# Layer norm statistics summed on four column tiles, kept as 128x128, and spread by selector matmuls

## What is computed

```
def _ln_t(v, eps=1e-05):
    m = jnp.mean(v, axis=-1, keepdims=True)
    s = jnp.var(v, axis=-1, keepdims=True)
    return (v - m) / jnp.sqrt(s + eps)
...
x = _L0_conv_ref(x, ...)                 # group norm, attention, residual
t = _to_tokens(x)                        # (8, 1024, 256)
t = t + _L1_attn_ref(_ln_t(t), ...)      # layer norm 0, causal attention
t = t + _L1_ffn_ref(_ln_t(t), ...)       # layer norm 1, top 2 of 32 experts
```

## Time and profile before

| | us |
|---|---|
| median of 3 executions | 3855.47 (3851.91 to 3858.39) |
| the profiled execution | 3846.6 |
| its span, first to last instruction | 3844.9 |
| PE busy | 3322.6 (86%) |
| DVE busy | 2186.7 (57%) |
| ACT busy | 1670.4 (43%) |
| mean granted TensorE clock | 0.896 of 2.4 GHz |

### The profile page before, as it was taken

How to read it: one execution, slowest core, us unless ns; L and a number is a source line. 1 busy time by engine, 2 the same in 40 slices (tenths; PEclk the granted TensorE clock), 3 DMA queues, 4 the chain that set the end, 5 groups by cost and what they waited for, 6 DMA issues and landing times.

```text
span 3844.9 us, 54190 instructions
## 1 busy us (share of the span) xinstructions
PE 3322.6 (86%) x17874; PEld 1820.9 (47%) x17874; DVE 2186.7 (57%) x2905; ACT 1670.4 (43%) x2604; POOL 425.7 (11%) x539
## 2 busy tenths in 40 slices
PE   5898799987998879988799788997889988899779
PEld 2344464435644356344563445534465344554347
DVE  6634585356843568445674447744567355773544
ACT  1454335533364333644236342463424634355333
POOL 0000030001300013000230002200022000320005
PEclk7798899988999889989899888998979989899889
DMA  3011340114402144021530205302142021421125
GB/s 99 1 45 34 90 137 28 45 34 110 139 7 52 26 123 126 11 57 26 140 106 17 61 18 140 99 17 61 29 138 88 18 61 43 143 70 34 45 57 165
DMA packets 151942, 263.02 MB, mean 68 GB/s; under 512 B 26832, under 2 KB 28880, under 8 KB 151504
## 3 DMA queue, kind: packets, MB, share of 16 engines
q1 hardware_dynamic: 151632, 259.15, 24.8%
HBM read 145.80 MB, written 9.44 MB: 40 GB/s over the span
## 4 chain that ended last, share of the span: by engine, by line
PE 61%; issue 14%; DVE 12%; ACT 7%; SPq 3%; DMA 2%; POOL 1%; DVEq 0%; ACTq 0%; POOLq 0%
PE ps_acc L592 8%; PE ps_two L705 7%; PE ps_one L544 7%; DVE tops L1072 6%; PE ps_two L669 6%; PE ps_acc L604 6%; PE ps_one L546 5%; PE ps_one L545 5%; PE ps_acc L544 3%; PE ps_acc L545 3%; PE ps_acc L546 3%; PE ps_one L705 3%; ACT probs L879 2%; SPq L457 2%; PE ps_two L686 1%
## 5 line engine op out<-in xcount | busy, mean ns | idle before, releaser
L1072 DVE TENSOR_REDUCE tops<-ps_two 128x2 bf16<-128x1024 f32 (+3 forms) x896 | 964.0, 1112 | 415.0 <-PE ps_two L669 247.2
L879 ACT ACTIVATE probs<-ps_two 128x1024 f32<-128x1024 f32 (+1 forms) x704 | 641.6, 961 | 234.4 <-PE ps_two L705 151.6
L669 PE MATMUL ps_two<-stacks 32*128 32x512 f32 (+3 forms) x1792 | 425.1, 506 | 178.0 <-DVE tops L1072 141.8
L705 PE MATMUL ps_two<-stacks 97*128 97x512 f32 (+3 forms) x1408 | 472.9, 442 | 67.8 <-ACT probs L879 37.7
L592 PE MATMUL ps_acc<-probs,v_sb 128*32 128x512 f32 (+3 forms) x3584 | 459.7, 587 | 0.0
L519 POOL TENSOR_TENSOR nat<-expert_sb,nat 128x256 fp32r<-128x256 f32 x512 | 386.3, 756 | 654.8 <-ACT nat L819 557.1
L705 PEld LDWEIGHTS ps_two<-stacks 97*128 97x128 f32 x1408 | 243.3, 196 | 357.4 <-ACT probs L879 184.7
L669 PEld LDWEIGHTS ps_two<-stacks 32*128 32x128 f32 x1792 | 171.5, 202 | 453.7 <-DVE tops L1072 237.0
L819 ACT CAST nat<-expert_sb 128x256 fp32r<-128x256 f32 x256 | 103.4, 407 | 630.3 <-DVE probs L1181 519.6
L604 PE MATMUL ps_acc<-probs,ones 128*32 128x512 f32 (+3 forms) x2944 | 358.4, 560 | 0.0
L525 POOL TENSOR_TENSOR act_lo<-xn,act_hi 128x2048 fp32r<-128x2048 f32 x8 | 36.1, 4511 | 2757.0 <-ACT act_hi L929 2757.0
(11 more groups left out here) (131 smaller groups left out, 4504.6 us busy)
## 6 DMA issues: line engine op xcount, KB each, us to landing
stacks<-nat SPq DMA_DIRECT2D x792, 128.0 KB, 2.4
expert_sb<-experts_dram SPq DMA_DIRECT2D x256, 256.0 KB, 2.8
probs<-gates_dram SPq DMA_DIRECT2D x512, 128.0 KB, 3.0
x_in<-x_in_dram SPq DMA_DIRECT2D x9, 1024.0 KB, 4.9
out_dram<-x_res SPq DMA_DIRECT2D x16, 512.0 KB, 2.9
probs<-mats_dram SPq DMA_DIRECT2D x1, 2048.0 KB, 9.3
gates_dram<-w_turn SPq DMA_DIRECT2D x64, 16.0 KB, 1.6
sel_w<-sel_dram SPq DMA_DIRECT2D x1, 32.0 KB, 8.4
```

The costliest lines, as they stand in the source:

```text
L669: mm = pe.matmul(acc[:, HALF * e:HALF * e + n_keys], q_st[rows, g, j, P * i:P * i + P], k_st[rows, g, j, HALF * kh:HALF * kh + n_keys], st ...
L705: mm = pe.matmul(at[:, a:HALF], k_st[0:MID + 1, g, j, P * k:P * k + P], q_st[0:MID + 1, g, j, HALF * hf + a:HALF * hf + HALF], start=True, ...
L879: done(act.activation(probs[:, n % 2, per * i:per * i + per, a:HALF], acc[:, :, a:HALF], ACT.Exp, scale=SCALE), s + (i,))
L1072: done(dve.reduce_max(tops[:, kh, 2 * pr:2 * pr + 2, i], acc[:, :, 0:cols(st, i, kh)], AX_X), s)
```

## The change

Each layer norm becomes four steps. "lna" sums the channels with column tiles: for each quarter q of the 512 tokens, `mean_w[:, 0:32]` is multiplied by 128 columns of `x_res` into partitions 32q to 32q+31 of the bank, so the 512 means lie on a 128x128 tile, each in 32 partitions. DVE copies it to `var_sb`, now 128x128. The new step "lnm" spreads it to 128x512 by four selector matmuls (`quarter_w`, 1/32 on the 32 rows of quarter q), and DVE subtracts and ACT squares as before. "lnb" sums the squares by column tiles; epsilon, ln, exp and the Newton step work on 128x128. The new step "lnr" spreads the roots by selector matmuls, and DVE multiplies `xn` by the bank. The new semaphore `scaled` tells PE that the roots are ready. Lines of the new kernel: `by_quarter` L625, `spread_out` L632, DVE copy L1151, subtractions L1157 and L1158, epsilon L1160, Newton step L1164 to L1167, multiplications L1173 and L1174.

```diff
--- before.py
+++ after.py
@@ -114,7 +114,7 @@
         steps += a[:1] + ([("down", 1)] if experts else []) + a[1:] + b[:1] + [("norm", 0, 0, 0), b[1], ("div", 0, 0, 0), b[2], ("fin", 0, 0, 0)] + b[3:]
 
         steps += c[:1] + [("norm", 0, 1, 0), c[1], ("div", 0, 1, 0), c[2], ("fin", 0, 1, 0), c[3]] + self.out(0, 0)
-        steps += [c[4], ("lna", 0, 0), c[5], ("lnb", 0, 0), c[6], c[7], ("parts", 0)]
+        steps += [c[4], ("lna", 0, 0), ("lnm", 0, 0), c[5], ("lnb", 0, 0), c[6], ("lnr", 0, 0), c[7], ("parts", 0)]
         steps += d[:1] + [("norm", 0, 0, 1), d[1]] + self.qk(1, 0, [0]) + [("div", 0, 0, 1), d[2], ("fin", 0, 0, 1)]
         t = rows_later(self.top(1, 0, 0))
         steps += d[3:5] + spread(d[5:8] + self.v(1)[:2], t)
@@ -122,8 +122,8 @@
         e, f, g, h = (self.mix(1, g, hf, hf == g) for hf in (0, 1) for g in (0, 1))
         t = rows_later(self.top(1, 1, 0))
         steps += e[:1] + [("norm", 0, 1, 1)] + self.qk(1, 1, [0]) + [("div", 0, 1, 1), e[1], e[2], ("fin", 0, 1, 1)]
-        steps += [e[3]] + t[:3] + self.out(0, 1) + t[3:8] + [("lna", 0, 1)] + t[8:]
-        steps += f[:1] + [("norm", 1, 0, 0), ("lnb", 0, 1), f[1], f[2], ("parts", 1), ("div", 1, 0, 0)]
+        steps += [e[3]] + t[:3] + self.out(0, 1) + t[3:8] + [("lna", 0, 1)] + t[8:9] + [("lnm", 0, 1)] + t[9:]
+        steps += f[:1] + [("norm", 1, 0, 0), ("lnb", 0, 1), f[1], ("lnr", 0, 1), f[2], ("parts", 1), ("div", 1, 0, 0)]
         steps += self.qk(1, 0, [1]) + [("fin", 1, 0, 0)] + self.v(1)[2:]
         steps += spread([f[3]] + self.qk(1, 1, [1]), rows_later(self.top(1, 0, 1)))
         m = [g[1], ("div", 1, 1, 0), g[2], ("fin", 1, 1, 0)] + g[3:]
@@ -131,10 +131,10 @@
         steps += g[:1] + [("norm", 1, 1, 0)] + spread(m[:-1], t[:-1]) + [m[-1], t[-1]]
 
         steps += h[:1] + [("norm", 1, 0, 1), h[1], ("div", 1, 0, 1), h[2], ("fin", 1, 0, 1), ("stats",), h[3]]
-        steps += self.out(1, 0) + [("gn",), h[4], ("lna", 1, 0), h[5], ("split", 0), ("lnb", 1, 0), h[6], h[7]]
+        steps += self.out(1, 0) + [("gn",), h[4], ("lna", 1, 0), ("lnm", 1, 0), h[5], ("split", 0), ("lnb", 1, 0), h[6], ("lnr", 1, 0), h[7]]
         steps += [("norm", 1, 1, 1), ("div", 1, 1, 1)] + self.qk(0, 0, [0]) + [("fin", 1, 1, 1)] + self.v(0)[:2]
         steps += self.out(1, 1)
-        steps += [("split", 1), ("lna", 1, 1)] + self.qk(0, 0, [1]) + [("lnb", 1, 1)]
+        steps += [("split", 1), ("lna", 1, 1), ("lnm", 1, 1)] + self.qk(0, 0, [1]) + [("lnb", 1, 1), ("lnr", 1, 1)]
         return steps
 
     def last(self):
@@ -147,8 +147,8 @@
     return s[1] == 0 and s[3] == 0 and s[4] in (1, 2, 4, 5, 6)
 
 
-LINKS = {"stats": 3, "gn": 8, "div": 2, "lna": 1, "lnb": 5, "logits": 5}
-N_CONSTS = 15
+LINKS = {"stats": 3, "gn": 8, "div": 2, "lnm": 1, "lnb": 3, "lnr": 1, "logits": 5}
+N_CONSTS = 18
 
 
 def events(steps):
@@ -167,7 +167,7 @@
     for s in steps:
         kind = s[0]
         add(kind, s)
-        if kind in ("gn", "qk", "v", "out", "lna", "lnb", "logits", "turn", "up"):
+        if kind in ("gn", "qk", "v", "out", "lna", "lnm", "lnb", "lnr", "logits", "turn", "up"):
             use("one", s)
         if kind == "mix" and added_up(s):
             add("add", s)
@@ -285,6 +285,7 @@
         mean_w = sb("mean_w", [P, P])
         block_w = sb("block_w", [P, P])
         ones32 = sb("ones32", [P, HD])
+        quarter_w = sb("quarter_w", [P, PH, P])
 
         x_in = sb("x_in", [P, CT, T])
         x_res = sb("x_res", [P, CT, T])
@@ -302,7 +303,7 @@
         tops = sb("tops", [P, NH, G, TT], BF16)
         rsum = sb("rsum", [P, HALF])
         o_sb = sb("o_sb", [P, HALF])
-        var_sb = sb("var_sb", [P, HALF])
+        var_sb = sb("var_sb", [P, P])
         rstd = sb("rstd", [P, HALF])
         st6 = sb("st6", [P, CT, NH, 6])
         mv = sb("mv", [P, CT, 2])
@@ -366,6 +367,7 @@
         att_hi = sem("att_hi")
         att_lo = sem("att_lo")
         squared = sem("squared")
+        scaled = sem("scaled")
         gates = sem("gates")
         gates_out = sem("gates_out")
         gate_in = [sem(f"gate_in{n}") for n in range(RING)]
@@ -494,7 +496,8 @@
             pool.memset(block_w[:], 1.0 / NORM_GROUP).then_inc(consts, 1)
             pool.memset(mean_w[:], 1.0 / C).then_inc(consts, 1)
             pool.memset(ones32[:], 1.0).then_inc(consts, 1)
-            pool.wait_ge(consts, 8)
+            pool.memset(quarter_w[:], 1.0 / HD).then_inc(consts, 1)
+            pool.wait_ge(consts, 9)
             for m, value in ((ident, 1.0), (ident_bf, 1.0), (minus_bf, -1.0)):
                 pool.affine_select(out=m[:], in_=m[:], compare_op=ALU.not_equal, fill=value, base=0,
                                    pattern=[[-1, P]], channel_multiplier=1).then_inc(consts, 1)
@@ -507,7 +510,11 @@
             pool.affine_select(out=blocks, in_=blocks, compare_op=ALU.is_ge, fill=0.0, base=0,
                                pattern=[[-NORM_GROUP, P // NORM_GROUP], [0, NORM_GROUP]],
                                channel_multiplier=1).then_inc(consts, 1)
-            pool.wait_ge(consts, 14)
+            pool.affine_select(out=quarter_w[:], in_=quarter_w[:], compare_op=ALU.is_ge, fill=0.0, base=0,
+                               pattern=[[-HD, PH], [0, P]], channel_multiplier=1).then_inc(consts, 1)
+            pool.wait_ge(consts, 16)
+            pool.affine_select(out=quarter_w[:], in_=quarter_w[:], compare_op=ALU.is_ge, fill=0.0, base=HD - 1,
+                               pattern=[[HD, PH], [0, P]], channel_multiplier=-1).then_inc(consts, 1)
             pool.affine_select(out=blocks, in_=blocks, compare_op=ALU.is_ge, fill=0.0, base=NORM_GROUP - 1,
                                pattern=[[NORM_GROUP, P // NORM_GROUP], [0, NORM_GROUP]],
                                channel_multiplier=-1).then_inc(consts, 1)
@@ -610,6 +617,20 @@
                             mm = pe.matmul(ps_acc[HD * j:HD * j + HD, 1, :], ones32[:], psums[:, j, :],
                                            start=False, stop=True)
                     mm.then_inc(mixed, 1)
+
+                def by_quarter(acc, columns):
+
+                    for k in range(CT):
+                        for q in range(PH):
+                            mm = pe.matmul(acc[HD * q:HD * q + HD, 0:P], mean_w[:, 0:HD], columns(k, P * q),
+                                           start=(k == 0), stop=(k == CT - 1))
+                    return mm
+
+                def spread_out(acc, quarters):
+
+                    for q in range(PH):
+                        mm = pe.matmul(acc[:, P * q:P * q + P], quarter_w[:, q, :], quarters[:, 0:P], start=True, stop=True)
+                    return mm
 
                 def times_down(hf, j):
 
@@ -731,16 +752,16 @@
 
                         for ct in range(CT):
                             read(("out", ln, hf, ct))
-                        acc = bank(s)
-                        for k in range(CT):
-                            mm = pe.matmul(acc, mean_w[:], x_res[:, k, half(hf)], start=(k == 0), stop=(k == CT - 1))
-                        filled(mm, s)
+                        filled(by_quarter(bank(s), lambda k, a: x_res[:, k, HALF * hf + a:HALF * hf + a + P]), s)
+                    elif kind == "lnm":
+                        read(("lna",) + s[1:])
+                        filled(spread_out(bank(s), var_sb), s)
                     elif kind == "lnb":
                         pe.wait_ge(squared, sec.value("lnb", sec.no["lnb"][s]))
-                        acc = bank(s)
-                        for k in range(CT):
-                            mm = pe.matmul(acc, mean_w[:], squares[:, k, :], start=(k == 0), stop=(k == CT - 1))
-                        filled(mm, s)
+                        filled(by_quarter(bank(s), lambda k, a: squares[:, k, a:a + P]), s)
+                    elif kind == "lnr":
+                        pe.wait_ge(scaled, sec.value("lnr", sec.no["lnr"][s]))
+                        filled(spread_out(bank(s), rstd), s)
                     elif kind == "logits":
                         pe.wait_ge(xn_ready, sec.value("lnb", 0))
                         acc = bank(s)
@@ -900,7 +921,7 @@
                         act.wait_ge(att_ready, sec.value("div", sec.no["norm"][("norm",) + s[1:]]))
                         act.activation(act_hi[:, g, half(hf)], rsum[:], ACT.Identity,
                                        bias=bias[:, 4 * st + 2, g:g + 1]).then_inc(att_hi, 1)
-                    elif kind == "lna":
+                    elif kind == "lnm":
                         _, ln, hf = s
                         read(s)
 
@@ -917,7 +938,7 @@
                             act.wait_ge(xn_ready, sec.value("lnb", lnb_seen - 1))
 
                         act.wait_ge(att_ready, sec.value("div", div_seen))
-                        inverse_root(rstd[:], var_sb[:], ln_root)
+                        inverse_root(rstd[:, 0:P], var_sb[:], ln_root)
                     elif kind == "parts":
                         hf = s[1]
```

(24 more changed lines are left out.)

## The result

The changed kernel takes 3897.4 us at the median of 7 runs (3877.3 to 3931.0), the kernel before 3855.8 us (3851.9 to 3861.4): a ratio of 1.0107, 95% interval 1.0069 to 1.0144. It is slower, as forecast, but by 42 us instead of 20, and the time lies just outside the range that was given (3843 to 3895). The seven runs of the changed kernel lie 54 us apart, those of the kernel before beside it 10 (in the larger groups of the experiments, 14 to 35 runs, 22 to 53), and they follow TensorE's mean granted clock: 3877.3 us at 0.886, 3897.4 at 0.875, 3931.0 at 0.869. The profiled execution is that slowest one, 84 us above the profiled one of the kernel before, so what its profile shows as lost is twice what the medians lost.

The account below looks back on a forecast made before the run. PE, busy 86% of the span, bounds the kernel, so its waits for layer norms matter. 8 x (-0.3 + 0 + 0.1) + 7 x 3.0 + 0.8 = +20 us: 3867 profiled, 3875.5 median; range 3843 to 3895.

Parts of the forecast that it names:

- Elsewhere: Rest of the kernel: constants covered by PE's start-up, no DMA changes form, SP's queue moves with the steps; nothing.
- the end of the sum at (1, 1): Time at the fourth place was counted from the norm's sum to the start of "logits", 18.9 us before, 22 forecast.
- (0,0): First layer-norm place of an image: PE's path and earlier exponentials give -0.3 us per image, bounds -0.6 and +1.
- (1,0): Third place: selectors add +1.1 us, but PE's later 3.05 us wait for DVE covers them; +0.1 us per image.
- Pieces: Costs per norm: selectors 0.12 us each, PE work 3.6 to 3.0 us, 128x128 steps 0.29 on DVE, 0.31 on ACT.
- rival 3: fp32 weight loads pace the selectors at full clock, 0.21 us each: +34 us on top, 3909 us; chance 0.12.
- (0,1): Second place: earlier chain at full clock against a possible further low-clock stretch; taken as 0, bounds -2.5 and +1.5 us.
- (1,1): Fourth place: -0.7 us at unchanged clock, but idle PE drops to low clock: +3.0 us per loop pass, 0.8 last image.
- Rival 1: Clock keeps its pattern, so DVE's shorter chain decides: -15 us, 3840 us; chance 0.20.

Follow-up runs that it names:

- pad_new_00: new_00 with 200 already-met waits added in PE's idle start, against the kernel before: 3859.6 us, ratio 1.0011.
- new_00: New scheme at (0,0) alone, the other three places as in the kernel before: 3890.7 us, ratio 1.0124.
- pad_after: The changed kernel with 256 already-met waits ahead of PE's first work: 3880.5 us, 1.0051 of the kernel before.
- new_01_c: New scheme at (0,1) alone, the other places as in the kernel before: 3856.4 us, ratio 0.9983.
- new_10: New scheme at (1,0) alone, the other places as in the kernel before: 3855.6 us, ratio 1.0010.
- new_11: New scheme at (1,1) alone, the other three places as in the kernel before: 3854.1 us, ratio 1.0010.
- shift_2: The kernel before with two extra 128x512 matmuls on PE ahead of the sum at (0,0): 3875.2 us, ratio 1.0038.
- fill_11: The changed kernel with 18 unused matmuls an image filling PE's two waits at (1,1): 3869.4 us, 1.0044 of the kernel before.
- pad_before: The kernel before with 328 already-met waits ahead of PE's first work: 3885.4 us, ratio 1.0061.

## Why the prediction was right and wrong

The forecast was +20 us, the result is +42, 2 us above the range. The steps that failed are "Elsewhere", which put the rest of the kernel at nothing, and the end of the sum at (1, 1). The loss lies in the first (in the profiles +38 and +21 us from (0,0) to (1,0), nearly all in steps that the change doesn't touch), the forecast lay in the second.

**Pieces: right.** Selectors 0.115 us each (0.12 forecast; 0.21 of rival 3 doesn't occur at the full clock), the PE work of a norm 2 x (0.6 + 0.92) = 3.0 us; DVE 0.29, ACT 0.31. Rival 3 falls.

**(0,0): the path right, the step "elsewhere" wrong.** The first product behind the sum comes at 18.95 us instead of 19.10, -0.15 where -0.3 was forecast, and pad_new_00 is level with the kernel before. But the prediction priced instructions by their time only. It said of the rest "SP's queue moves with the steps", and nothing of where PE's longer code would lie. At (0,0) alone 24 matmuls with their loads stand in the place of four; the ends of its blocks move, and one of them meets the twelve DMA issues 60 to 70 us behind. That is 1.1% in new_00 (41 us, of which 37 are gone in pad_new_00), and 0.6% of the changed kernel's 1.1% (pad_after; by the two intervals 0.1 to 1.0%).

**(0,1): right.** 0 forecast, new_01_c 0.9983 (0.9961 to 1.0005). Its profiled execution, its slowest, has 421 us of the low level from (0,1) to (1,0) instead of 346 and takes 986 us there instead of 965, so this is a statement on the total only.

**(1,0): the cover right, the clock left out.** +0.1 us forecast. At an equal clock it is -0.2 (27.24 us in new_10 instead of 27.40): the 3.05 us wait did absorb the selectors. But the wait ahead of "lnr" is 2.26 us where 1.3 was put. The chain from the epsilon to the roots takes 2.3 us as forecast, but DVE starts it only behind the subtraction of "split". No fall of the clock was counted here, and new_10 has nine more in eight images than the kernel before, 51 us of the low level instead of 20. So in all kernels with the scheme there the stretch behind grows by 1.1 to 1.6 us an image (225 to 229 us in eight images, in the other kernels 211 to 223). Alone it costs nothing in the total (new_10).

**(1,1): the mechanism right, the sum wrong.** "lnm" 3.5 us behind the sum (forecast 3.7), both rounds at the low level, "logits" at 23.3 us where 22 was forecast: +4.7 a pass instead of +3.0. Of the difference 0.9 us is the wait for the roots, 3.19 us instead of 2.3, because DVE reads a bank of "qk" first. The term that failed is the end of the sum. It stopped at the start of "logits" and so left them as long as before, at 0.50; the level rose to the full one and they gave 3.8 back. Net 0.9 a pass in the two profiles, and new_11 can't be told from no change (+5 us, interval -5 to +12) instead of being at +22. The sum's sign came true for another reason than it gave.

**Chances.** Rival 1 (the clock keeps its pattern) supposed that a pattern is a matter of the edited stretch. shift_2 shows that it isn't: 0.43 us more per image of PE's work in a place without waits costs 18.8 us in all, 5 to 23 by the interval. A range that takes only the edited places into account is too narrow for this kernel: shifts of this size alone cost 0.4 and 0.7%. That the result missed the range by only 2 us, with the sign right, is luck.

**What stays open.** About half of the changed kernel's loss is settled: the late stacks. The other half goes with the clock (113 us more of the low level in pad_after), of which (1,1)'s waits are a part that fill_11 shows. Why two or three places together have the worse pattern, why a shift without any late stack costs three to five times its own time, and why new_00 has more falls of the clock also some 15 us ahead of the late stacks, is not settled by any run.

## What to carry to other kernels

Before a step on PE is priced, look at what PE's clock does at the waits around it, and carry the sum on until the level is the same again in both: what is lost at one wait may be given back by the next group. An edit that changes the length of PE's code can slow a DMA issue elsewhere; compare the source view of the DMA issues (who waited for them) before and after, and move the code by some waits in an idle start before judging the edit. Where PE waits for 1 to 2 us on others many times in a loop, fillers somewhat shorter than the wait, into a bank already granted, can pay more than shortening the chain: 2.2% here, against a loss of 1.1% by the change itself. Where the bank is what PE waits for, they can't.

## What was not expected of the hardware

- A 16 KB instruction transfer that meets a run of 0.60 us DMA issues makes one of them longer, up to 1.95 us in new_00 and in pad_before (the eighth of twelve in both). The issue alone doesn't tell the harm: in two images of new_00 the longest is 0.75 us, and PE still waits 1.37 us for the stack.
- The clock's falls are at the same few places behind the sum of each image, to some tenths of a us: in new_00 at 53.6 to 54.0 us in five images, at 41.5 to 41.6 in two. With 0.43 us of work more an image (shift_2) the low level over the whole run is 54 us longer.
- A met wait in PE's program isn't free: the 328 of pad_before run from 10.0 us, when their semaphore stands at its value, to 27.5 us, 53 ns each; the 256 of pad_after from 10.0 to 23.6, the same 53 ns.
- Executions of one kernel differ by 54 us of 3900 (the changed kernel, seven runs, mean clock 0.869 to 0.886), and the kernel before by as much when it runs often enough (32 runs on one chip: 3827 to 3880 us, clock 0.887 to 0.901).
